# One-hots, sums and node work of a graph kernel moved ahead of VectorE's wait for the gathered rows

## The chip, the cores and the metric

The kernel runs on one core of a Trainium2 chip. The metric is the device time of one execution in microseconds (us); the median of three runs is shown, and one more execution was taken by the hardware profiler. Engines: TensorE (PE, its weight loads PEld), VectorE (DVE), ScalarE (ACT), GpSimd (POOL), and SyncE (SP), which issues most DMAs.

## The reference, cut to what matters

6250 nodes with 128 features, 200000 edges sorted by destination. Two layers, each on the layernorm of the features, each added to them:

```python
h = relu(layernorm(x))
# layer 0: graph attention, 4 heads of 32
xp = h @ W;  e = leaky_relu(a_s[src] + a_d[dst], 0.2)
m = segment_max(e, dst);  e = exp(e - m[dst])
out = segment_sum(e * xp[src], dst) / segment_sum(e, dst)
x = x + relu(out + bias)
# layer 1: edge features and neighbour sums
h = relu(layernorm(x))
edge_agg = segment_sum(edge_attr @ We + be, dst)
x_comb = concat([h, edge_agg]);  neigh = segment_sum(x_comb[src], dst)
x = x + relu((x_comb + neigh) @ W1 + b1) @ W2 + b2
```

The self loops of layer 0 are in the start values of the sums.

## The kernel before, in words

A preparation (0 to 126 us) makes a table of `xp` with its logits in DRAM. Then a loop over 87 groups of 2304 edges (128 partitions by J = 18), two buffers, the same `item(n, b, it)` written once for each engine. Last comes a phase of 49 windows that multiplies an adjacency matrix with the projected nodes (from 2668 us), which the change does not touch.

In one group the engines do this:

- GpSimd gathers the rows of the 2304 sources with 18 indirect DMAs (line 816) into `V[b]`. It runs one group ahead of the others, but holds back by itself (`yield_to_chain`, line 788): ahead of gather 6 it waits for the carry matmul of the group before, ahead of 8 for the peaks (`mg_b`), ahead of 11 for the lookup, ahead of 14, 15 and 16 for the three thirds of the weighted sums (`vm_b`).
- VectorE waits for the 18 gathers (line 1637) and starts the chain of the group, which makes the running maximum per destination: copy of the logits (1638), scan `pre1` (1643), a transpose by TensorE (1142), scan `tails` over the partitions (1651), a matmul back (1144), carry (1660), scan `pre2` (1664), peaks (1671), split of them into three bf16 parts (`split_peaks`, 1507 to 1513). TensorE multiplies the peaks with the one-hots `selH` (1161, 18 matmuls). VectorE makes the new maximum and the shift of the window's 128 nodes out of it (1689 to 1717), also split in parts. TensorE looks the shift up for each edge (1177, 18 matmuls), VectorE forms the exponent (1725 to 1737), ScalarE the exponential (949), VectorE multiplies the rows with it in three parts (1742), TensorE sums them (1194).
- `select` (1479, 1491) makes `selH`, the one-hots of each edge's node in its window, for the sums; it waits until the one-hots of the group before have been used. ScalarE copies them to float32 (`SEL`, line 933), behind its evacuation of three adjacency blocks, and TensorE takes them for the sums of the edge features (1133: three of the eighteen ahead of the lookup, the rest behind it) and of the rows (1194).
- `rescale_state` and `add_sums` (1523, 1533) take the sums of the window before to the new maximum and add the group's; they wait for the load of the window's sums, for the fold factor and for the last third of the matmuls. SyncE then stores the sums (509).
- `finish_weights` to `finish_shift` (1543 to 1610) are some twenty small steps of the nodes of the group before (m = n - 1): mean, bias, residual, layernorm with a Newton square root. Each waits for the one before (`done`). `finish_projection` (1612) evacuates the projection of the group n - 2; it waits for its matmuls and until the store of the projection before has landed (`y_out`), since both use the tile `fy`. Before, these steps stand one by one between the chain's steps.
- `edge_marks` (1493) make one-hots for the adjacency matrix, which TensorE multiplies (1123, 1125) and ScalarE evacuates; SyncE stores 1568 KB of it for each group (526).

SyncE's queue of a group n, in order: store of the sums n - 1, store of the peaks n, loads of the indices n + 2, of peaks and rows n + 1, of the edge features n + 2 (1152 KB, line 453, after the edge-feature sums of n), of the sums n (502, after the transposes of window n - 1), of x (505), stores of the residual n - 1 (515), of the projection n - 2 (520), of the adjacency n - 1 (526).

The order of work is written out by hand; engines meet only through semaphores.

Of the kernel before, what the change touches and what calls it, by code (L numbers as in the profile page):

```python
# [14 lines left out]
H = 4  # L15
# [37 lines left out]
NK = 3  # L53
# [28 lines left out]
def gnn_kernel(nc, x, src, dst, attr, W, att_src, att_dst, bias0, We, be, W1, b1, W2, b2, out):  # L82
    ctx = ExitStack()
    with ctx:
# [81 lines left out]
        step = sb("step", [128, RT])  # L166
# [133 lines left out]
        def s(name):  # L300
            if name not in S:
                S[name] = sem(name)
            return S[name]
# [980 lines left out]
        def _(dve):  # L1284
# [194 lines left out]
            def select(n, b, extra_group=None):  # L1479
                after(dve, s("mg_b"), n, 1)  # L1480
                after(dve, s("selc_b"), n, 1)
                if extra_group is None:
                    at = drp[:, bass.DynSlice(n, 1), :].rearrange("p a j -> p (a j)")
                else:
                    v.tensor_scalar(drxp[b][:, :].rearrange("p (j e) -> p j e", e=2),
                                    dd[:, bass.DynSlice(extra_group, 1), :].rearrange("p a (j e) -> p (a j) e", e=1)
                                    .to_broadcast([128, J, 2]), exto[:, bass.DynSlice(n - NG, 1)], None,
                                    ALU.subtract).then_inc(s("drx_b"), 1)
                    dve.wait_ge(s("drx_b"), n - (NG - 1))
                    at = drxp[b][:, :]  # L1490
                equal(selH, J, WIN, at).then_inc(s("sel_b"), 1)
# [41 lines left out]
            def add_sums(n, b):  # L1533
                dve.wait_ge(s("vm_b"), n * QN + QN)
                dve.wait_ge(s("ms_b"), n * 2 + 2)
                v.tensor_tensor(state[:, :], state[:, :], pv[b][:, 0:ST], ALU.add).then_inc(s("merged"), 1)
# [82 lines left out]
            def item(n, b, it, g=None):  # L1619
# [5 lines left out]
                def between(step, *more):  # L1625

                    if m is not None:
                        step(m, *more)
# [7 lines left out]
                                -BIG, None, ALU.mult).then_inc(s("cont_b"), 1)  # L1636
                dve.wait_ge(s(f"gat{b}"), it * 16 * J + 16 * J)
# [8 lines left out]
                select(n, b, extra_group)  # L1646
                if m is not None:
                    rescale_state(m, 1 - b)
# [4 lines left out]
                if m is not None:  # L1653
                    add_sums(m, 1 - b)
                if not (is_extra or (isinstance(n, int) and n < 2)):
                    finish_projection(n - 2)
                between(finish_weights)
                between(finish_mean)
# [3 lines left out]
                between(finish_bias)  # L1662
# [4 lines left out]
                between(finish_residual)  # L1667
                last = isl[:, bass.DynSlice(g, 1), :].rearrange("p a (j c) -> p (a j) c", c=1)
                v.tensor_copy(peaks[:, :, NK * H:NK * H + 1], last).then_inc(s("pkl_b"), 1)
# [3 lines left out]
                between(finish_stats)  # L1673
                split_peaks(n, 0)
                between(finish_variance)
                split_peaks(n, 1)
                between(finish_eps)
                split_peaks(n, 2)
                between(finish_halve)
                split_peaks(n, 3)  # L1680
                between(finish_guess)
# [3 lines left out]
                between(finish_b2)  # L1685
                between(newton_square, 0)
# [6 lines left out]
                between(newton_factor, 0)  # L1693
# [5 lines left out]
                between(newton_step, 0)  # L1699
# [5 lines left out]
                between(newton_square, 1)  # L1705
# [3 lines left out]
                between(newton_factor, 1)  # L1709
                split_shift(n, b, 0)  # L1710
                between(newton_step, 1)
                split_shift(n, b, 1)
                between(newton_square, 2)
                split_shift(n, b, 2)
                between(newton_factor, 2)
# [3 lines left out]
                between(newton_step, 2)  # L1719
                between(finish_shift)  # L1720
# [172 lines left out]
```

## Time and profile before

| | us |
| --- | --- |
| median of 3 runs | 3113.4 (3105.56 to 3114.23) |
| profiled execution, own time | 3102.13 |
| its span | 3100.2 |
| PE busy | 2043.0 (66%) |
| PE weight loads busy | 1674.9 (54%) |
| DVE busy | 1807.2 (58%) |
| ACT busy | 1085.6 (35%) |
| POOL busy | 1673.2 (54%) |

The profile is one execution. Busy times are shares of the span; no engine is near all of it. Times in a timeline are from the start of the span. "Idle before" is the time in which an engine did nothing just ahead of an instruction, with the one that ended it. The granted clock (PEclk) is a share of 2.4 GHz. The ends of matmuls are modelled.

### The profile page before, as it was taken

The page shows a single profiled execution, that of the slowest core. Times are in us where ns is not written, and L with a number is a line of the kernel's source. Part 1 is how long each engine was busy: PE and PEld are TensorE (multiplying, and loading weights), DVE is VectorE, ACT ScalarE, POOL GpSimd, SP SyncE. Part 2 cuts the span into 40 slices and gives each one's busy share as a digit, 9 for nine tenths or more (in the row PEclk, how much of TensorE's full clock was granted, in tenths as well). Part 3 has the DMA queues.
Part 4 walks back from the last instruction along what each step waited for, and adds up shares of the span by engine and source line. Part 5 has one row for each costly group of instructions (what it writes and reads, how often), then busy time and mean ns, then how long its engine had stood idle before and what let it go on. Part 6 is the DMA issues. An engine that isn't in the chain of part 4 may idle for free.

```text
span 3100.2 us, 64216 instructions
## 1 busy us (share of the span) xinstructions
PE 2043.0 (66%) x16208; PEld 1674.9 (54%) x16208; DVE 1807.2 (58%) x6198; ACT 1085.6 (35%) x2295; POOL 1673.2 (54%) x1626
## 2 busy tenths in 40 slices
PE   4365665665665655665656656656656656699998
PEld 3354554554554544554545545545545544588887
DVE  7566676665666666666666766766766766411111
ACT  3134344344434443443443443443444443300000
POOL 4566666666666666666666666666666666000000
PEclk8677777776777767777767777777777777799999
DMA  9855655655655555655556556556556555666654
GB/s 192 134 163 177 194 168 174 195 159 180 193 155 187 177 169 189 189 160 185 162 176 194 157 184 194 168 173 194 156 185 194 156 185 176 225 213 214 225 212 146
DMA packets 276907, 560.29 MB, mean 181 GB/s; under 512 B 113395, under 2 KB 211139, under 8 KB 248081
## 3 DMA queue, kind: packets, MB, share of 16 engines
q1 hardware_dynamic: 226763, 444.37, 42.5%
q0 software_dynamic: 50112, 115.56, 16.5%
q8 instruction: 12, 0.20, 0.0%
q14 instruction: 20, 0.16, 0.0%
HBM read 382.53 MB, written 177.22 MB: 181 GB/s over the span
## 4 chain that ended last, share of the span: by engine, by line
PE 41%; issue 20%; DVE 15%; DMA 9%; another core or an unknown queue 5%; SPq 3%; ACT 2%; POOL 2%; ACTq 1%; DVEq 1%; POOLq 0%
PE pv L1133 10%; PE pv L1248 9%; DMA big<-table,idx 8%; PE pv L1194 7%; PE pt L1248 4%; PE pt L1123 3%; PE pm L1161 2%; POOL big L816 2%; ACT xsb L852 2%; PE pa L1123 1%; DVE peaks L1513 1%; DVE tabb L1477 1%; PE pa L1177 1%; ACTq L905 1%
## 5 line engine op out<-in xcount | busy, mean ns | idle before, releaser
L816 POOL DMA_INDIRECT big<-table,idx x1566 | 1639.8, 1047 | 929.9 <-issue 414.2
L852 ACT ACTIVATE xsb<-pt 128x343 f32 x1042 | 477.8, 459 | 1213.3 <-PE pt L1125 567.1
L1133 PE MATMUL pv<-big 128*128 128x128 f32 x3132 | 523.6, 336 | 5.7 <-ACT big L852 3.5
L1133 PEld LDWEIGHTS pv<-big 128*128 128x128 f32 x3132 | 490.3, 246 | 36.1 <-issue 11.7
L1123 PE MATMUL pt<-tabb 128*128 128x343 bf16 x1042 | 400.0, 384 | 65.8 <-ACT xsb L852 36.5
L1194 PE MATMUL pv<-big 128*128 128x133 f32 x3132 | 391.3, 280 | 7.0 <-DVE big L1742 4.2
L1638 DVE COPY logit<-big 128x72 f32<-128x72 f32 x87 | 21.9, 252 | 608.6 <-DMA big<-table,idx 540.1
L1194 PEld LDWEIGHTS pv<-big 128*128 128x128 f32 x3132 | 367.8, 190 | 16.2 <-DVE big L1742 8.6
L1477 DVE TENSOR_TENSOR tabb<-iotah,keyp 128x2064 bf16<-128x2064 bf16 x261 | 319.7, 1225 | 0.0
L1142 PE MATMUL pm<-ident,pre 128*4 128x128 f32 x87 | 32.5, 374 | 433.9 <-DVE pre L1643 226.5
L1248 PE MATMUL pv<-big,xsb 128*128 128x384 bf16 (+1 forms) x1617 | 279.3, 330 | 18.5 <-DVE big L1779 18.5
L852 ACT ACTIVATE xsb<-pa 128x343 f32 x521 | 238.9, 458 | 95.0 <-ACT xsb L852 50.3
L1248 PEld LDWEIGHTS pv<-big,xsb 128*128 128x128 bf16 (+1 forms) x1617 | 230.4, 147 | 52.4 <-issue 21.4
L1142 PEld LDWEIGHTS pm<-ident,pre 128*4 128x4 f32 x87 | 7.2, 82 | 451.5 <-DVE pre L1643 236.4
L1742 DVE TENSOR_TENSOR big<-big,pm 128x768 f32<-128x768 f32 x261 | 233.4, 949 | 26.2 <-ACT pm L852 18.7
L1125 PE MATMUL pt<-tabb 128*128 128x49 bf16 x1041 | 224.9, 216 | 0.0
L1123 PE MATMUL pa<-tabb 128*128 128x343 bf16 x521 | 200.8, 385 | 28.3 <-issue 18.3
L1161 PE MATMUL pm<-peaks,selb 128*128 128x13 bf16 x1566 | 56.2, 174 | 228.8 <-DVE peaks L1513 143.7
L1123 PEld LDWEIGHTS pt<-tabb 128*128 128x128 bf16 x1042 | 114.9, 110 | 159.5 <-ACT xsb L852 63.1
L1161 PEld LDWEIGHTS pm<-peaks,selb 128*128 128x128 bf16 x1566 | 48.5, 105 | 261.2 <-DVE peaks L1513 157.2
L852 ACT ACTIVATE big<-selb 128x2304 f32<-128x2304 bf16 x87 | 184.1, 2116 | 1.0 <-DVE selb L1477 1.0
L852 ACT ACTIVATE fhT<-pt,b1s 128x128 f32<-128x128 f32 (+1 forms) x49 | 18.0, 367 | 388.6 <-PE pt L1225 388.6
(289 smaller groups left out, 2975.8 us busy)
## 6 DMA issues: line engine op xcount, KB each, us to landing
adj<-xsb SPq DMA_DIRECT2D x87, 1568.0 KB
big<-in_edge_attr_dram SPq DMA_DIRECT2D x87, 1152.0 KB
xsb<-adj SPq DMA_DIRECT2D x33, 1568.0 KB, 6.2
selb<-rel SPq DMA_DIRECT2D x87, 576.0 KB
tabb<-adj SPq DMA_DIRECT2D x16, 1568.0 KB, 6.2
big<-table,idx POOLq DMA_INDIRECT x1566
state<-sums SPq DMA_DIRECT2D x87, 130.5 KB
sums<-state SPq DMA_DIRECT2D x87, 130.5 KB
```

The source lines that it names most:

```text
L816: pool.indirect_dma_start(out=V[b][:, j, 0:rows], out_offset=None, in_=table, in_offset=bass.IndirectOffsetOnAxis(ap=index[b][:, j:j + 1], ...
L852: return nc.scalar.activation(out_, in_, func, **kw).then_inc(s(name), 1)
L905: _, at = nc.values_load_multi_w_load_instructions(offs[0:1, bass.DynSlice(n * OW + lo, hi - lo)], engines=[mybir.EngineType.Activation], ...
L1123: ins = nc.tensor.matmul(pab[c % 3], ohl[:, c, :], ohk[:, c, 0:KW], start=True, stop=alone)
L1125: ins = nc.tensor.matmul(pab[c % 3][:, 0:NB], ohl[:, (c - 1) % J, :], ohc[:, (c - 1) % J, 0:NB], start=False, stop=True)
L1133: ins = nc.tensor.matmul(sumA[b], SEL[b][:, j, :], AT[b][:, j, :], start=(j == 0), stop=(j == J - 1))
L1142: nc.tensor.transpose(tailT, pre1[:, :, J - 1], ident[:, :]).then_inc(s("tailT_b"), 1)
L1161: ins = nc.tensor.matmul(mg, selH[:, j, :], peaks[:, j, :], start=(j == 0), stop=(j == J - 1))
L1194: ins = nc.tensor.matmul(sumV[b], SEL[b][:, j, :], V[b][:, j, 0:TAB], start=(j == 0), stop=(j == J - 1))
L1248: ins = nc.tensor.matmul(pay[k][0:rows, 0:NK * C], adjT[k][:, 0:rows, h], yb[:, h, :], start=(h == 0), stop=(h == NB - 1))
L1477: return v.tensor_tensor(to.rearrange("p j (w e) -> p j w e", e=2), v_in, at, ALU.is_equal)
L1742: v.tensor_tensor(v4, v4, wps[:, js, :].rearrange("p j (h a) -> p j h a", a=1) .to_broadcast([128, QUART, H, F]), ALU.mult).then_inc(s("vw ...
```

## The change

In VectorE's `item`, the one-hots, the copy of the last flags, the rescaling and adding of the sums of the group before, the projection and all the finishing steps are taken out of the chain and stand in one block ahead of the wait for the gathered rows. The chain's own instructions and their order, and the programs of the other engines, stay as they are.

```diff
                                 -BIG, None, ALU.mult).then_inc(s("cont_b"), 1)
+                select(n, b, extra_group)
+                last = isl[:, bass.DynSlice(g, 1), :].rearrange("p a (j c) -> p (a j) c", c=1)
+                v.tensor_copy(peaks[:, :, NK * H:NK * H + 1], last).then_inc(s("pkl_b"), 1)
+                if m is not None:
+                    rescale_state(m, 1 - b)
+                    add_sums(m, 1 - b)
+                if not (is_extra or (isinstance(n, int) and n < 2)):
+                    finish_projection(n - 2)
+                for step in (finish_weights, finish_mean, finish_bias, finish_residual, finish_stats,
+                             finish_variance, finish_eps, finish_halve, finish_guess, finish_b2):
+                    between(step)
+                for r in range(3):
+                    between(newton_square, r)
+                    between(newton_factor, r)
+                    between(newton_step, r)
+                between(finish_shift)
                 dve.wait_ge(s(f"gat{b}"), it * 16 * J + 16 * J)
...
-                select(n, b, extra_group)
-                if m is not None:
-                    rescale_state(m, 1 - b)
                 after(dve, s("thru_c"), n)
                 after(dve, s("tailT_b"), n)
...
-                if m is not None:
-                    add_sums(m, 1 - b)
-                if not (is_extra or (isinstance(n, int) and n < 2)):
-                    finish_projection(n - 2)
-                between(finish_weights)
-                between(finish_mean)
                 after(dve, s("cback_b"), n)
...
-                between(finish_bias)
...
-                between(finish_stats)
                 split_peaks(n, 0)
-                between(finish_variance)
                 split_peaks(n, 1)
...
-                between(newton_step, 2)
-                between(finish_shift)
```

## Rows read from the trace of the kernel before

**Rows 1.** The page's costliest groups: line, engine, tiles, count | busy, mean | idle before.
```profile
L1638 DVE COPY logit<-big 128x72 f32<-128x72 f32 x87 | 21.9, 252 | 608.6 <-DMA big<-table,idx 540.1
```
**Rows 2.** Source view of line 1638: durations in ns, first and last start in us.
```profile
L1638 DVE COPY logit<-big x87: 211/220/455, 126.2 to 2633.2; 128x72 f32<-128x72 f32 x87
```
**Rows 3.** Timeline of a period's first part: start, duration in us, engine, line, tiles.
```profile
1528.42 0.22 DVE L1638 COPY logit<-big 128x72 f32<-128x72 f32 x1 [8.10 <-DMA big<-table,idx]
...
1528.98 1.34 DVE L1477 TENSOR_TENSOR selb<-iotah,drp 128x2304 bf16<-128x2304 bf16 x1
1529.12 0.38 PE L1142 MATMUL pm<-ident,pre 128*4 128x128 f32 x1 [5.24 <-DVE pre L1643]
...
1530.51 0.40 DVE L1651 TENSOR_TENSOR_SCAN tails<-thruT,pm 4x128 f32<-4x128 f32 x1
...
1530.97 0.59 PE L1144 MATMUL pm<-ident,tails 4*128 4x4 f32 x2 [1.48 <-issue]
...
1533.82 2.12 ACT L852 ACTIVATE big<-selb 128x2304 f32<-128x2304 bf16 x1
...
1534.29 0.65 PE L1161 MATMUL pm<-peaks,selb 128*128 128x13 bf16 x18 [1.63 <-DVE peaks L1511]
...
1536.18 1.62 PE L1133 MATMUL pv<-big 128*128 128x128 f32 x6 [0.24 <-ACT big L852]
...
1538.29 0.66 PE L1177 MATMUL pa<-node,selb 128*128 128x24 bf16 x18 [0.49 <-DVE node L1511]
...
1539.76 4.87 PE L1133 MATMUL pv<-big 128*128 128x128 f32 x30
```
**Rows 4.** Timeline of the same and the next period: GpSimd's gathers, SyncE's issues, VectorE's wait.
```profile
1529.27 1.88 POOL L816 DMA_INDIRECT big<-table,idx  x1 [0.30 <-issue]
...
1547.21 0.33 SPq L502 DMA_DIRECT2D state<-sums  x1
...
1549.79 0.18 DVE L1635 TENSOR_SCALAR cont<-isl 128x68 f32 x1
...
1549.87 0.35 SPq L520 DMA_DIRECT2D sums<-fy  x1
...
1550.77 0.94 POOL L816 DMA_INDIRECT big<-table,idx  x1 [0.37 <-issue]
...
1551.19 0.33 SPq L526 DMA_DIRECT2D adj<-xsb  x1
...
1557.36 0.22 DVE L1638 COPY logit<-big 128x72 f32<-128x72 f32 x1 [7.39 <-DMA big<-table,idx]
```
**Rows 5.** Windows: stretch, length, busy of the engines, PEclk, DMA share, GB/s.
```profile
1527.00:1541.00 14.00, 8.04 (x69) 5.75 (x70) 10.84 (x51) 5.46 (x9) 9.91 (x9) 0.50 0.36 75
1549.00:1557.00 8.00, 2.80 (x22) 1.56 (x20) 0.98 (x4) 4.01 (x10) 6.12 (x6) 0.94 1.01 390
```
**Rows 6.** Timeline of the first group, which has no node work.
```profile
128.46 0.58 PE L1144 MATMUL pm<-ident,tails 4*128 4x4 f32 x2 [0.83 <-DVE tails L1651]
129.09 0.22 DVE L1660 SCALAR_TENSOR_TENSOR logit<-pm,cin,logit 128x4 f32<-128x4 f32 x1 [0.68 <-PE pm L1144]
...
131.25 0.63 PE L1161 MATMUL pm<-peaks,selb 128*128 128x13 bf16 x18 [2.20 <-DVE peaks L1513]
```
**Rows 7.** Groups by line of VectorE from 1499 to 2601 us, 38 periods.
```profile
L1689 DVE TENSOR_SCALAR pen<-pm 128x1 f32<-128x1 f32 x38 | 6.0, 157 | 26.2 <-remote 14.3 <-PE pm L1161 11.3
```
**Rows 8.** Timeline behind the last group: adding, projection and finishing with no chain between.
```profile
2653.21 0.43 DVE L1536 TENSOR_TENSOR state<-state,pv 128x261 f32<-128x261 f32 x1 [2.44 <-PE pv L1194]
2653.55 0.34 DVE L1616 SCALAR_TENSOR_TENSOR fy<-bew,fdeg,pa 128x128 f32<-128x128 f32 x1
...
2658.28 0.16 DVE L1609 SCALAR_TENSOR_TENSOR fnm<-fmv,fy 128x1 f32<-128x1 f32 x1
```
**Rows 9.** Tile view of `state`: landing of its loads whose landing the trace has.
```profile
DMA to landing us min/median/max: 1.7/5.4/12.2
```
**Rows 10.** Timeline of another group: the same thirty attribute rows.
```profile
2617.80 3.59 PE L1133 MATMUL pv<-big 128*128 128x128 f32 x30
```

More of the change, by code:

```diff
@@ L1666, in item @@
                     .then_inc(s("pre2_b"), 1)
-                between(finish_residual)
-                last = isl[:, bass.DynSlice(g, 1), :].rearrange("p a (j c) -> p (a j) c", c=1)
-                v.tensor_copy(peaks[:, :, NK * H:NK * H + 1], last).then_inc(s("pkl_b"), 1)
                 after(dve, s("pre2_b"), n)
@@ L1672, in item @@
                                 last.to_broadcast([128, J, H]), ALU.mult).then_inc(s("pk_b"), 1)
-                between(finish_stats)
                 split_peaks(n, 0)
-                between(finish_variance)
                 split_peaks(n, 1)
-                between(finish_eps)
                 split_peaks(n, 2)
-                between(finish_halve)
                 split_peaks(n, 3)
-                between(finish_guess)
                 if not is_extra:
@@ L1684, in item @@
                     v.tensor_scalar(selT, selT, ranko[:, 0:1], None, ALU.is_equal).then_inc(s("selt_b"), 1)
-                between(finish_b2)
-                between(newton_square, 0)
                 after(dve, s("mg_b"), n)
@@ L1692, in item @@
                                 AX.X, ALU.add).then_inc(s("mgs_b"), 1)
-                between(newton_factor, 0)
                 dve.wait_ge(s("st_load"), n * 32 + 32)
@@ L1698, in item @@
                     .then_inc(s("mnew_b"), 1)
-                between(newton_step, 0)
                 after(dve, s("mnew_b"), n)
@@ L1704, in item @@
                                 ALU.add).then_inc(s("nu_b"), 1)
-                between(newton_square, 1)
                 after(dve, s("nu_b"), n)
@@ L1708, in item @@
                                        op0=ALU.mult, op1=ALU.max).then_inc(s("sh_b"), 1)
-                between(newton_factor, 1)
                 split_shift(n, b, 0)
-                between(newton_step, 1)
                 split_shift(n, b, 1)
-                between(newton_square, 2)
                 split_shift(n, b, 2)
-                between(newton_factor, 2)
                 split_shift(n, b, 3)
```

## The prediction, made before the change was run

> **What bounds the kernel now.** I read the costliest groups first. VectorE's copy of the gathered logits (line 1638) has the largest idle time that an engine spends ahead of one VectorE line: 608.6 us over 87 groups, 7.0 us a group, nearly all of it until the gather landed [rows 1]. So VectorE, busy 58% of the span, is no bound by its sum. Then the source view of that line: its first and last starts are 126.2 and 2633.2, so 86 periods take 2507.0 us, 29.15 us each [rows 2]. The rest of the span (preparation, adjacency phase) is not touched.
>
> Then the timeline of one period. The rows land, VectorE starts the chain (logit, scan, TensorE round trip, tails, round trip, carry, scan, split), TensorE multiplies the peaks (1161), VectorE finishes the shift, TensorE looks it up (1177), weights follow, sums follow, and GpSimd is allowed its last two gathers only behind those sums. In the period from 1528.42 to the next logit copy at 1557.36 the reader is to see three stretches: 9.87 us to TensorE's lookup (1177 at 1538.29), 11.4 us to the end of VectorE's own list (mask of line 1635 at 1549.79), and 7.6 us in which VectorE waits [rows 3, 4]. That last stretch is a DMA stretch: the 16 engines are at a share of 1.01 and 390 GB/s from 1549 to 1557, with the adjacency store issued at 1551.19 [rows 4, 5]. The period is a closed loop: what leaves the first stretch shortens it, and what is put into the last is free only up to 7.6 us and only if its inputs are there.
>
> **The first stretch without the moved work.** Now: copy 1528.42, the transpose (1142) 0.70 later, tails at 2.09, the back matmul (1144) at 2.55, 1161 at 5.87 [rows 3]. Between the transpose's end (1.08) and the tails stand the one-hots (1.34 us) and the rescaling. Without them the tails wait only for the transpose. The first group gives the delay: it has no node work, and its carry starts 0.63 after a 0.58 us matmul row, 0.05 after the end [rows 6]. So tails at 1.08 + 0.05 = 1.13; back matmul 0.46 later (as now) 1.59; carry 0.63 later 2.22; and 1161 starts 131.25 - 129.09 = 2.16 after the carry in that first group: 4.38. The gain there is 5.87 - 4.38 = 1.49 us. Of this the one-hots and rescaling are 0.96; the some twenty small steps give only the rest, because each stood in the gap in which the next step of the chain waited for the one before. I take nothing for the Newton steps behind the peaks for that reason (bounds: nothing, and 0.16 us each for the last two, ahead of the edge marks, which the wait for the lookup covers anyway).
>
> The lookup has a second path. ScalarE's copy of the one-hots (2.12 us) started 2.85 behind the back matmul (1533.82), because the evacuation of three adjacency blocks stands ahead of it; then six attribute rows (1536.18) and the lookup [rows 3]. It moves by 0.96 only: copy at 4.44, attribute sums 2.36 later at 6.80, lookup at the earliest 1.62 later at 8.42. By the VectorE path it is 9.87 - 1.49 = 8.38. So the lookup starts at 8.42, and **1.4 us** are gained. Making the one-hots sooner doesn't help that copy: it is held by what stands ahead of it on ScalarE.
>
> Bounds: VectorE also waits ahead of line 1689, 26.2 us over 38 groups, 0.69 us each, partly for nothing that the view names [rows 7]. If such waits end at fixed moments and so fill up what the chain gives, the floor is 1.4 - 0.7 = 0.7 us; if they vanish, the gain is 1.4 + 0.7 = 2.1 us. I keep them as they are.
>
> **The last stretch with the moved work.** Ahead of the wait now come one-hots, copy of the last flags, rescaling, adding, projection, finishing, shift. The end of the last group shows this block alone: adding 2653.21, projection 2653.55, shift 2658.28 with 0.16 [rows 8], so 5.2 us from adding, 4.9 from projection to the end; every step waits for the one before with nothing between. One-hots and rescaling are 1530.51 - 1528.98 = 1.53 us [rows 3]. From 1549.90: adding at 1551.5 at the earliest, all done at 1556.8, 0.6 before the copy at 1557.36. It fits by 0.6 us if nothing is late, but two inputs are young. Rescaling waits for the state load of that group, issued at 1547.21, and the projection waits until the store of the projection before has landed (it shares the tile), issued at 1549.87 [rows 4]. The nearest landing row is that of the state loads: 1.7 least, 5.4 median, 12.2 most [rows 9], the median behind a 1568 KB load. This state load stands behind 1152 KB, which by size makes 5.4 x 1152/1568 = 4.0: 1551.2, in time. For the 64 KB store I take 3 us, nearer to the least, since it stands behind small transfers: 1552.87, projection there instead of 1551.85, block done at 1557.8, the copy 0.4 late. By the bounds the store costs nothing at 1.7 us and 1555.3 + 4.9 = 1560.2, 2.8 us late, at 5.4.
>
> The one-hots now run while GpSimd makes the last two gathers. The row of a gather begun at 1529.27 is 1.88 us long: it ends 0.83 behind the one-hots of 1528.98 to 1530.32, where an undisturbed one takes 0.94 [rows 3, 4]. Moved to 1549.90 to 1551.24 they meet the gather of 1550.77, whose end goes from 1551.71 to 1552.07: 0.36 us (bounds 0 and 0.94). The Trainium skill, page "SBUF — State Buffer", section "Who interferes with whom", has it that a tensor_tensor with both inputs in SBUF only takes the pair's read side and so should leave descriptor making alone (which it calls inferred); by it this term is nothing. The row of 1.88 us is against it, and the sum goes by the row.
>
> SP's queue: the store of the sums (130 KB) leaves at about 1552 instead of 1531, that is into the full stretch. At 390 GB/s its 130 KB add 0.3 us to what has to be drained ahead of the rows. All other SP entries keep their order and gates, since load of sums, residual and projected stores stay behind the attribute load. The gathers' yields to the chain come sooner with the chain; GpSimd has 18 gathers of 0.94 + 0.30 us, 22.5 us, in a period of 28, so it stays under.
>
> These don't add: rows landing 0.4 to 0.6 later (gather and store) and VectorE 0.4 late are the larger of two. With the groups not being alike I take **0.6 us**.
>
> **The sum.** -1.4 + 0.6 = -0.8 us a group, over 86 groups -69 us. The profiled execution took 3102.1 us (3100.2 span), so 3033; the median of the runs shown is 11 us above that execution (3113.4), so 3044, and I say **3042 us**.
>
> **Rivals.**
> 1. The gain is given back: the rows land when the DMA queue is drained, and nothing but the start of that drain counts; or VectorE is late by 1 to 1.4 us. For it: share 1.01 in the stretch. Against: the adjacency store is issued behind attribute sums that shift with the lookup. Time 3113 less 0 to 0.3 x 86 = 3087 to 3113.
> 2. Slower: the projection's wait for the landed store, now ahead of the wait for the rows, decides. Everything of the chain queues behind it on VectorE, and TensorE, ScalarE and GpSimd behind that. Price: each us of landing beyond 2.6 is a us of every group; it decides beyond 2.6 + 1.4 = 4.0 us. At the 5.4 of the landing row [rows 9] the net is 2.8 - 1.4 = +1.4 us, +120 us: 3235; at 4.7, 3173. For it: the full DMA stretch; against: at 64 KB it is small, and the adjacency store is issued only behind it.
> 3. More is gained: the unnamed waits vanish and TensorE's clock rises sooner. From 1527 to 1541 it was granted 0.50 of full speed (1.2 GHz) [rows 5], and the thirty attribute rows took 4.87 us, against 3.59 in another group [rows 3, 10], which an earlier rise to 2.4 GHz would explain. With the first 0.7 and half of the second 1.28 a group gains 1.3 more: 112 us, 2930.
>
> **Chances.** Forecast 0.52 (its own range 2985 to 3085), rival 1 0.16, rival 2 0.14, rival 3 0.18. Less than 0.3% (9 us) can't be told from no change. Rival 1 is half faster, half same: faster 0.52 + 0.18 + 0.07 = 0.77, same 0.08, slower 0.15 (rival 2 and a late tail of rival 1). The range takes the forecast, rival 1 and the nearer half of rival 3: 2955 to 3120.
>
> **What would show it.** Right: 1161 starts about 4.4 and 1177 about 8.4 behind the logit copy (5.87 and 9.87 now); VectorE's idle ahead of line 1638's copy falls from 7.0 to under 1 us; the shift of line 1609 stands ahead of the copy; some gathers at the end of a group are 1.3 us long; a period near 28.3 us. Wrong: a gap of VectorE ahead of line 1616 (store) or 1528 (state) above 1.5 us and the gather landed well before the copy (rival 2), or the copy still waiting for rows with a period of 29 (rival 1), or full clock before 1177 (rival 3).

## The result and the profile after

The changed kernel takes 3134.61 us (median of 4 runs, 3130.25 to 3141.55), the kernel before 3112.24 us (4 runs, 3105.56 to 3114.23): ratio 1.0077, 95% interval 1.0052 to 1.0103. It is slower by 0.8%, where 3042 us was forecast. Two copies of one kernel, run side by side later, differed by 0.3%; the loss is small but clear of that. The profiled execution took 3130.25 us, its span is 3128.3 us.

The source view of the logit copy, now line 1654 (durations in ns; first and last start in us), answers to [rows 2]:
```profile
L1654 DVE COPY logit<-big x87: 206/220/410, 127.5 to 2662.0; 128x72 f32<-128x72 f32 x87
```
86 periods take 2534.5 us, 29.47 us each, against 29.15: 0.32 us more, 27.5 us in all, which is the whole difference of the spans (28.1 us). So the loss is in this loop.

A period's first part in the timeline, as in [rows 3] (the last brackets give the idle time before the row and what ended it):
```profile
1508.74 0.21 DVE L1654 COPY logit<-big 128x72 f32<-128x72 f32 x1
1509.42 0.37 PE L1142 MATMUL pm<-ident,pre 128*4 128x128 f32 x1 [5.09 <-DVE pre L1659]
1510.37 0.58 PE L1144 MATMUL pm<-ident,tails 4*128 4x4 f32 x2 [0.57 <-issue]
1511.09 0.22 DVE L1667 SCALAR_TENSOR_TENSOR logit<-pm,cin,logit 128x4 f32<-128x4 f32 x1 [0.78 <-PE pm L1144]
...
1513.12 2.12 ACT L852 ACTIVATE big<-selb 128x2304 f32<-128x2304 bf16 x1
1513.18 0.65 PE L1161 MATMUL pm<-peaks,selb 128*128 128x13 bf16 x18 [1.13 <-DVE peaks L1513]
1515.29 1.65 PE L1133 MATMUL pv<-big 128*128 128x128 f32 x6 [0.46 <-ACT big L852]
1516.74 0.16 DVE L1685 TENSOR_SCALAR pen<-pm 128x1 f32<-128x1 f32 x1 [2.91 <-remote]
...
1518.69 0.66 PE L1177 MATMUL pa<-node,selb 128*128 128x24 bf16 x18 [1.76 <-DVE node L1513]
```
The reader is to see that the chain did what it was to do as far as TensorE's peaks' matmuls: 1161 starts 4.44 us behind the logit copy (5.87 before, 4.38 forecast), ScalarE's copy 4.38 (4.44 forecast). Then VectorE waits 2.91 us for a product whose matmuls were over at 1513.83, and the lookup starts at 9.95: in this group nothing is left of the 1.43 us.

One group is a sample. The means over the 87 groups, in us behind the logit copy of the same group, say how much came through:

| | before | after | difference |
| --- | --- | --- | --- |
| peaks' matmuls start (1161) | 6.90 | 5.36 | -1.54 |
| penalty starts (1689, after: 1685) | 8.52 | 8.15 | -0.37 |
| lookup starts (1177) | 10.56 | 10.16 | -0.40 |
| VectorE's last instruction ahead of the moved block (mask, 1635) | 21.89 | 21.60 | -0.29 |
| from there to the next logit copy | 7.26 | 7.87 | +0.61 |
| period | 29.15 | 29.47 | +0.32 |

The chain up to the peaks is 1.54 us shorter, three quarters of that are lost ahead of the penalty, 0.29 us are left at the mask, and the longer list behind it costs 0.61.

The waits behind this stand in the groups by line (busy, mean ns | idle before). First of the kernel before, then of the changed kernel:
```profile
L1725 DVE TENSOR_REDUCE lks<-pa 128x144 f32<-128x432 f32 x87 | 52.8, 607 | 69.5 <-remote 68.5 <-PE pa L1177 0.9
L1689 DVE TENSOR_SCALAR pen<-pm 128x1 f32<-128x1 f32 x87 | 13.7, 157 | 66.8 <-remote 40.3 <-PE pm L1161 24.9
```
```profile
L1712 DVE TENSOR_REDUCE lks<-pa 128x144 f32<-128x432 f32 x87 | 52.9, 608 | 98.9 <-remote 98.8
L1685 DVE TENSOR_SCALAR pen<-pm 128x1 f32<-128x1 f32 x87 | 13.8, 159 | 203.1 <-remote 188.5 <-PE pm L1161 14.3
...
L1528 DVE TENSOR_TENSOR state<-state,fold 128x128 f32<-128x128 f32 x87 | 25.4, 292 | 41.3 <-DMA state<-sums 39.1 <-issue 2.1
L1616 DVE SCALAR_TENSOR_TENSOR fy<-bew,fdeg,pa 128x128 f32<-128x128 f32 x87 | 29.9, 344 | 6.5 <-PE pa L1114 2.9 <-DMA sums<-fy 2.5
L1654 DVE COPY logit<-big 128x72 f32<-128x72 f32 x87 | 21.1, 242 | 5.0 <-DMA big<-table,idx 4.1 <-issue 0.6
```
The wait ahead of the penalty grew from 0.77 to 2.33 us a group ((203.1 - 66.8)/87 = 1.57 more), that ahead of the lookup's sums from 0.80 to 1.14. (Before, VectorE still had steps of the nodes to do while TensorE multiplied the peaks, so a part of the same delay did not show as idle time.) VectorE's wait for the rows, 608.6 us before [rows 1], is down to 5.0: what fills it is the moved list, with 0.47 us a group of waiting for the loaded state (41.3/87) in it, and at most 0.07 ahead of the projection (6.5/87, of it 0.03 for the store).

The load of the state, the list's end and the next copy in the timeline (as [rows 4]), and the two windows that answer to [rows 5] (stretch, length, busy of PE, PEld, DVE, ACT, POOL, PEclk, DMA share, GB/s):
```profile
1527.43 0.33 SPq L502 DMA_DIRECT2D state<-sums  x1
...
1530.10 0.19 DVE L1635 TENSOR_SCALAR cont<-isl 128x68 f32 x1
1530.21 1.35 DVE L1477 TENSOR_TENSOR selb<-iotah,drp 128x2304 bf16<-128x2304 bf16 x1
...
1532.59 0.29 DVE L1528 TENSOR_TENSOR state<-state,fold 128x128 f32<-128x128 f32 x1 [0.92 <-DMA state<-sums]
...
1538.14 0.16 DVE L1609 SCALAR_TENSOR_TENSOR fnm<-fmv,fy 128x1 f32<-128x1 f32 x1
...
1538.26 0.24 DVE L1654 COPY logit<-big 128x72 f32<-128x72 f32 x1
```
```profile
1507.00:1521.00 14.00, 7.66 (x67) 5.34 (x68) 8.56 (x33) 5.35 (x9) 9.27 (x10) 0.50 0.32 72
1530.00:1538.00 8.00, 2.57 (x20) 1.35 (x18) 6.38 (x29) 3.64 (x9) 5.67 (x6) 0.74 1.00 370
```
The copy follows the list at once: VectorE is late. From the mask (1530.10) to the copy are 8.16 us, 7.57 before [rows 4]: 0.6 us more, the same as in the means. The rescaling (1528) starts 5.16 us behind the issue of the load that it waits for. VectorE does 2.3 us less in the first window, and the stretch isn't shorter.

### The profile page after: what moved, and what is told of

It is laid out like the page before. It is cut to its first block, busy times and chain, and to the rows that moved or that the text cites. A ratio compares the mean times of both kernels' runs of the same rounds, so it can differ in the third digit from the quotient of the medians.

```text
span 3128.3 us, 64216 instructions
## 1 busy us (share of the span) xinstructions
PE 2081.7 (67%) x16208; PEld 1712.1 (55%) x16208; DVE 2014.1 (64%) x6198; ACT 1078.0 (34%) x2295; POOL 1657.4 (53%) x1626
## 4 chain that ended last, share of the span: by engine, by line
PE 38%; issue 19%; DVE 18%; another core or an unknown queue 9%; DMA 5%; SPq 4%; ACT 4%; ACTq 2%; DVEq 0%; POOL 0%; POOLq 0%
PE pv L1133 11%; PE pv L1248 8%; PE pv L1194 6%; PE pt L1248 4%; ACT xsb L852 3%; DMA state<-sums 2%; PE pt L1123 2%; DVE selb L1682 2%; ACTq L905 1%; DVE tabb L1477 1%; PE pa L1177 1%; PE pa L1123 1%; PE pm L1144 1%; DVE pre L1670 1%
## 5 line engine op out<-in xcount | busy, mean ns | idle before, releaser
L1133 PE MATMUL pv<-big 128*128 128x128 f32 x3132 | 561.3, 353 | 34.3 <-ACT big L852 17.6
L1133 PEld LDWEIGHTS pv<-big 128*128 128x128 f32 x3132 | 527.7, 263 | 70.9 <-issue 34.0
L1194 PEld LDWEIGHTS pv<-big 128*128 128x128 f32 x3132 | 367.9, 190 | 6.4 <-DVE big L1729 2.3
L1779 DVE TENSOR_TENSOR fy<-pa,fxw 128x128 f32<-128x128 f32 (+1 forms) x49 | 14.3, 292 | 227.3 <-PE pa L1232 227.3
```

The lines of the kernel that those rows point to most:

```text
L1133: ins = nc.tensor.matmul(sumA[b], SEL[b][:, j, :], AT[b][:, j, :], start=(j == 0), stop=(j == J - 1))
L1194: ins = nc.tensor.matmul(sumV[b], SEL[b][:, j, :], V[b][:, j, 0:TAB], start=(j == 0), stop=(j == J - 1))
```

## The experiments

They ran in five lots on five different chips, beside the kernel before, which took 2838, 3114, 3170, 3176 and 2848 us there. I call the first and the last the fast chips, the others the slow ones. No chip was used twice, so these runs can't tell the chip from the occasion. Ratios hold within a lot.

**First lot: where the peaks' result is waited for.** GpSimd's pause for that result was moved in both kernels, since it is ahead of gather 8 and the stall ended soon behind gather 7 (where VectorE waited over 0.5 us, 1.9 us behind the gather's end in the median); the one-hots were moved alone; and two Newton rounds were left out of the changed kernel (the reciprocal root is then less exact).
```diff
 # after_y4, before_y4: yield_to_chain
-                if j == 6:
-                    pool.wait_ge(s("cback_b"), n)
-                    pool.sem_inc(s("g_started"), 1)
-                if j == 8:
+                if j == 4:
                     pool.wait_ge(s("mg_b"), n)
 # sel_only: before, with only this moved
+                select(n, b, extra_group)
                 dve.wait_ge(s(f"gat{b}"), it * 16 * J + 16 * J)
 ...
-                select(n, b, extra_group)
 # after_newton1: FIN = 12
-                for r in range(3):
+                for r in range(1):
```


> The changed kernel with GpSimd's yield for the peaks put ahead of gather 4 instead of gather 8 (and the carry's yield dropped, which it implies), so that far fewer gathers are in flight while TensorE multiplies the peaks. In the changed kernel line 1161 starts 5.4 us (least 4.33) after the logit copy, and VectorE's line 1685 that takes its result starts at 8.2, though the matmuls are 0.65 us long. Theory A, the gathers in flight hold back what the engines tell each other: line 1685 comes down to 5.6 to 6.2 us after the copy, and the period falls from 29.5 by 1 to 2 us (time 2960 to 3060). Theory B, the result is late for a reason of TensorE's own (its clock, its weight loads) : line 1685 stays at 8 to 8.3 and the time stays within 10 us of 3135 or goes up. Theory C, ScalarE's copy of the one-hots out of the tile that TensorE reads: the same as B here, since the copy stays at 4.4 to 6.5.

> The same shift of the yields in the kernel before. Line 1161 starts at 6.95 us on average (least 5.85) and line 1689 at 8.55. Theory A: line 1689 falls to 7.0 to 7.3 and the period by about 1 us, time near 3030; with the moved block still in the chain it stays above the changed kernel with the same yields by the 1.4 us a group that I had predicted. Theories B and C: line 1689 stays at 8.5, the time within 10 us of 3112 or above.

> The kernel before with one part of the change: only the one-hots (select) stand ahead of the wait for the rows, everything else stays in the chain. It takes 1.3 us out between pre1 and tails and adds nothing that waits for a landing, and VectorE's block ahead of the wait is 1.3 us in 7.6. Theory A (the end of the peaks' wait is set from outside the chain): line 1161 starts about 1 us sooner, line 1689 hardly moves (8.2 to 8.5), and the time is 3090 to 3115, less than the changed kernel's because VectorE is not late for the rows. Theory B (the chain sets it): 3020 to 3050.

> The changed kernel with one Newton round instead of three (two rounds of the square root are left out), so its block ahead of the wait is six dependent steps, 1.27 us, shorter. If VectorE's lateness for the rows (copy 1.18 us after the gather's store has landed, 0.62 before the change) is what made the change a loss, the idle time ahead of the logit copy comes back (0.3 to 0.6 us a group), the period falls by 0.4 to 0.6 us and the time to 3085 to 3100, below the kernel before. If the DMA queue alone sets the landing, the time stays within 10 us of 3135.

Measured, before at 2837.52 us: after_y4 2943.62 us, ratio 1.038 (1.036 to 1.041); before_y4 3007.02, 1.061 (1.058 to 1.063); sel_only 2762.65, 0.973 (0.971 to 0.976); after_newton1 2828.7, 0.998 (0.996 to 0.999). The surprise is the chip: the same kernel is 9% faster there, and VectorE has no stall ahead of the penalty in any of the four traces. Groups by line of sel_only:
```profile
L1689 DVE TENSOR_SCALAR pen<-pm 128x1 f32<-128x1 f32 x87 | 13.1, 150 | 0.0
```
So this lot could not test the stall; it shows that the moved pause makes the gathers late where there is nothing to repair, and that the one-hots alone are worth 2.7% there.

**Second lot: the parts, and both kernels again.** The finishing steps moved and the one-hots left in the chain (fin_ahead); one-hots, rescaling and adding moved and the finishing steps left (sel_sums).
```diff
 # fin_ahead: after, with
-                select(n, b, extra_group)
                 last = isl[:, bass.DynSlice(g, 1), :].rearrange("p a (j c) -> p (a j) c", c=1)
 ...
+                select(n, b, extra_group)
                 after(dve, s("thru_c"), n)
 # sel_sums: before, with ahead of the wait for the rows (and not behind it)
+                select(n, b, extra_group)
+                last = isl[:, bass.DynSlice(g, 1), :].rearrange("p a (j c) -> p (a j) c", c=1)
+                v.tensor_copy(peaks[:, :, NK * H:NK * H + 1], last).then_inc(s("pkl_b"), 1)
+                if m is not None:
+                    rescale_state(m, 1 - b)
+                    add_sums(m, 1 - b)
```


> The kernel before, unchanged, for its own trace on this chip. Its ratio is 1.000 under either theory. Theory A (the 1.4 us that the chain gained up to the peaks' matmuls is swallowed by stalls of several engines between the peaks' first matmul and the penalty on VectorE): if the time is near 2838 us, the stalls are absent from its trace (VectorE waits under 0.3 us for the peaks' result, the penalty starts 0.7 to 1.0 us after the peaks' first matmul, against 1.6 us in the trace of the prediction); if it is near 3112 us they are there. Theory B (the swallowing is a wait of this program for a fixed event, whatever the condition): the distance stays 1.6 us at any time.

> The changed kernel, unchanged. Theory A: where before takes near 2838 us there is no stall that could swallow the 1.4 us; the peaks' result is used 1.0 to 1.5 us earlier in the group, and what decides is only how late VectorE's longer list ends before the rows: with 0.6 us of lateness at its end the ratio is 0.97 to 0.99; where before takes near 3112 us it is 1.008 again. Theory C (VectorE's list of 18 steps and their writes end so late that the transfers and the matmuls behind them, and with them the last gathers, land 1 us late as well): the ratio is 1.00 to 1.02 on either chip, and the wait for the rows starts no earlier than before.

> The changed kernel with the one-hots back in the group's chain, behind the first scan (about 0.9 us of VectorE's chain); rescaling, sums and all finishing steps stay ahead of the wait. The select's move alone gave 0.973. Theory C (the list's length decides): this kernel's list ends 1.4 us sooner than after's, so it is 0.5 to 1.0% faster than the changed kernel. Theory A: the moves add up, so it is slower than the changed kernel by what the one-hots cost in the chain, 0.5 to 0.9 us a group, 1.5 to 2.5%.

> The one-hots, the last-column copy, the rescaling and the adding of sums ahead of the wait; the finishing steps of the last group stay between the chain's steps, as in the kernel before. Theory A: the steps that leave the chain are 4 of some 0.1 us each, so it is 0.3 to 1% faster than the move of the one-hots alone (0.973), unless the wait for the state's rows ends behind the gathered rows. Theory C: sums made sooner bring the writes forward and leave the list 1.5 us shorter than after's, ratio 0.96 to 0.975, clearly under the changed kernel.

Measured, before at 3113.8 us: before_same 3119.9 us, 1.003 (1.001 to 1.005), so 0.3% is what two copies of one kernel differ by; after_same 3134.07, 1.008 (1.006 to 1.011), the result again; fin_ahead 3145.09, 1.009 (1.005 to 1.013); sel_sums 3130.66, 1.008 (1.005 to 1.011). Every version that shortens the chain ends in the same place; neither theory had that, since C wanted both parts under the changed kernel and A wanted fin_ahead 1.5% or more above it. In sel_sums TensorE's peaks' matmuls start 4.7 us behind the copy, and one group shows who waits (timeline):
```profile
1515.72 0.65 PE L1161 MATMUL pm<-peaks,selb 128*128 128x13 bf16 x18 [1.33 <-DVE peaks L1513]
...
1516.88 0.94 POOL L816 DMA_INDIRECT big<-table,idx  x1 [0.31 <-issue]
...
1519.53 0.16 DVE L1688 TENSOR_SCALAR pen<-pm 128x1 f32<-128x1 f32 x1 [2.75 <-remote]
...
1519.67 0.46 ACT L852 ACTIVATE xsb<-pt 128x343 f32 x1 [2.10 <-remote]
...
1520.28 0.94 POOL L816 DMA_INDIRECT big<-table,idx  x1 [2.46 <-remote]
```
VectorE, ScalarE and GpSimd all wait for products of TensorE that were finished 1516.4 to 1517.4, and all go on within 0.8 us. It is the word of the finished work that comes late, not the work. What it waits for there the trace doesn't say ("remote" stands where it has no record of the event).

**Third lot: a fixed amount of events, or the gathers?** SyncE got 24 idle increments a group.
```diff
                     store_sums(n - 1, base_before)
+                    for _ in range(24):
+                        sp.sem_inc(s("sp_turn"), 1)
                 store_peak(n, b, base)
```


> The kernel before with 24 extra semaphore increments a group on SyncE, that nobody waits for, put where SyncE waits 5.8 us a group for the new peaks (506.2 us over 87 groups in the trace of before). They cost the data path nothing if each takes under 0.1 us. Theory D (where before takes near 3112 us, the stalls of several engines are set by a fixed amount of events that a group produces, such as semaphore updates and instruction ends, and not by the kernel's chain): the time rises there, by 1% or more, while where before takes near 2838 us it stays within 0.3%. Theory E (the stalls come from gathers in flight): no change within 0.3% on either.

> The move of the one-hots alone, again. It gave 0.973 where before takes near 2838 us. Theory A (the chip's condition swallows what the chain gains up to the peaks): 0.973 again where before takes near 2838 us, and 1.00 to 1.01 where it takes near 3112 us, with VectorE waiting 2 us or more for the peaks' result. Theory F (the longer list alone decides, and the one-hots alone are a gain anywhere): 0.97 to 0.98 on either.

> The changed kernel, unchanged, again. It gave 1.008 where before takes near 3112 us. Where before takes near 2838 us: theory A says 0.975 to 0.99 (no stall to swallow the gain, 0.5 to 1.0 us a group given back by the list's late end); theory C (the list's late end gives the whole gain back) says 1.00 to 1.01; its cut to one Newton round gave 0.998 there, so I take 1.00 to 1.01 for likelier.

> The changed kernel with GpSimd's wait for the peaks' result moved from ahead of gather 8 to ahead of gather 4, and its wait for the carry left out, again. It gave 1.038 where before takes near 2838 us, with the gathers late. Where before takes near 3112 us: theory E (gathers in flight hold up the peaks' result) says that the penalty starts within 1.5 us of the peaks' first matmul (3.0 us in the changed kernel's trace), ratio 0.99 to 1.02; theory D (a fixed amount of events a group) says that the group's period stays near 29.2 to 29.6 us, ratio 1.00 to 1.015, since the gathers' own bound of 27.3 us lies below it.

Measured, before at 3169.6 us: before_spinc 3178.07 us, 1.003 (1.001 to 1.005), no more than a copy of the kernel differs, so theory D is wrong at the size that it named; sel_only_2 3140.79, 0.991 (0.989 to 0.993); after_same_2 3153.48, 0.994 (0.992 to 0.997); after_y4_2 3461.08, 1.093 (1.091 to 1.095). On this chip the change is a small gain, and the one-hots alone a larger one. Theory A missed here too: it wanted 1.00 or more for the one-hots, with a wait of 2 us for the peaks' result, which was 0.95 us (82.8/87). after_y4_2 lies 7% above the range that I gave, but its rows say where the stall is. Groups by line:
```profile
L1709 DVE TENSOR_REDUCE lks<-pa 128x144 f32<-128x432 f32 x87 | 52.8, 607 | 187.9 <-remote 184.4 <-issue 3.5
L1682 DVE TENSOR_SCALAR pen<-pm 128x1 f32<-128x1 f32 x87 | 13.8, 159 | 2.6
```
With GpSimd halted ahead of gather 4 the wait ahead of the penalty is gone (2.6 us, 181.3 in after_same_2), and that ahead of the lookup's sums grew from 104.3 to 187.9 us: GpSimd now runs through ten gathers there (4 to 13). The stall went where the gathers went, but it doesn't last until they are over: of the 71 groups in which VectorE waits over 0.5 us ahead of the lookup's sums, 69 end their wait in the middle of a gather, and GpSimd gathers on. Ahead of the penalty GpSimd waits for the same word as VectorE, so that it has stopped there doesn't show that the stop ends the stall.

**Fourth lot: the run of gathers made shorter and longer.** The pause ahead of gather 6, and in after_late none until the one ahead of gather 11 (the wait for the carry ahead of 6 stays there, but gather 6 starts 1.28 us behind gather 5 in the mean, as without a wait).
```diff
 # before_y6, sel_y6, after_y6
                 if j == 6:
-                    pool.wait_ge(s("cback_b"), n)
-                    pool.sem_inc(s("g_started"), 1)
-                if j == 8:
                     pool.wait_ge(s("mg_b"), n)
 # after_late
-                if j == 8:
-                    pool.wait_ge(s("mg_b"), n)
-                    pool.sem_inc(s("g_started"), 1)
```


> The kernel before with one pause of GpSimd for the peaks' result, ahead of gather 6 (before: for the carry ahead of 6, for the peaks' result ahead of 8). Theory E (a run of gathers without a pause holds up all engines): where before takes 3112 us or more, the penalty starts 0.7 to 1.5 us behind the peaks' first matmul (1.6 us in before) and that matmul near 6.0 us, so the chain up to it is 1 to 1.5 us shorter, and gather 8 starts at about 9.3 us as before; ratio 0.96 to 1.00, less if a new stall comes behind the lookup. Theory G (the stall has its place for another reason): the penalty stays at 8.5 us and the gathers are 2 us later, ratio 1.02 to 1.06. Where before takes near 2838 us there is no stall, the gathers bound: 1.01 to 1.04.

> The same pause with the one-hots ahead of the wait for the rows. Theory E: where before takes 3112 us or more, the penalty at 5.7 to 6.5 us against 8.7 us, gather 8 at 8.5 us against 9.4 us, ratio 0.94 to 0.98, the fastest of the four. Theory G: the penalty stays past 8 us, ratio over 1.00. Where before takes near 2838 us: 0.97 to 1.00, against 0.973 with the pauses as they were.

> The same pause in the changed kernel. Theory E: where before takes 3112 us or more, the penalty at 5.1 to 5.8 us against 8.3 us in the changed kernel's trace, gather 8 at 8.0 us against 9.0 us, the rest of the group's chain 1 us or more ahead of it; the list that ends late then costs what it was to cost, so ratio 0.95 to 0.99. Theory G: the penalty stays past 8 us, ratio over 1.01. Where before takes near 2838 us: 1.00 to 1.03.

> The changed kernel without GpSimd's pause for the peaks' result: it gathers on to number 11, where it waits for the lookup's matmuls. Theory E: where before takes 3112 us or more, the stall lasts until gather 10 is done, so the penalty starts at 10 to 12 us against 8.3 us and the ratio is 1.02 to 1.08. Theory G: the penalty stays at 8.3 us and the gathers are earlier, ratio 0.97 to 1.00. Where before takes near 2838 us: no stall, gathers earlier, 0.96 to 1.00.

Measured, before at 3175.89 us: before_y6 3234.2 us, 1.017 (1.013 to 1.021); sel_y6 3179.17, 1.001 (1.000 to 1.003); after_y6 3367.48, 1.060 (1.056 to 1.065); after_late 3524.94, 1.109 (1.105 to 1.113). Idle of VectorE ahead of the penalty, groups by line of before_y6, sel_y6, after_y6 and after_late in this order:
```profile
L1686 DVE TENSOR_SCALAR pen<-pm 128x1 f32<-128x1 f32 x87 | 13.2, 151 | 1.5 <-remote 1.2 <-PE pm L1158 0.2
```
```profile
L1686 DVE TENSOR_SCALAR pen<-pm 128x1 f32<-128x1 f32 x87 | 13.2, 152 | 0.3 <-PE pm L1158 0.2
```
```profile
L1682 DVE TENSOR_SCALAR pen<-pm 128x1 f32<-128x1 f32 x87 | 13.8, 159 | 102.4 <-remote 54.9 <-PE pm L1158 46.9
```
```profile
L1682 DVE TENSOR_SCALAR pen<-pm 128x1 f32<-128x1 f32 x87 | 13.8, 158 | 578.7 <-remote 576.4 <-PE pm L1158 2.2
```
In the changed kernel that is, by the gather ahead of which GpSimd pauses, 0.03 us a group (4), 1.18 (6), 2.08 to 2.33 (8, three traces) and 6.65 (none until 11); with the one-hots alone 0.00 (6) and 0.95 (8), in the kernel before 0.02 (6) and 0.74 to 0.77 (8). A group of after_late, timeline and windows:
```profile
1527.76 0.65 PE L1158 MATMUL pm<-peaks,selb 128*128 128x13 bf16 x18 [3.85 <-DVE peaks L1510]
...
1530.22 0.94 POOL L813 DMA_INDIRECT big<-table,idx  x1 [0.30 <-issue]
1533.66 0.16 DVE L1682 TENSOR_SCALAR pen<-pm 128x1 f32<-128x1 f32 x1 [6.36 <-remote]
...
1533.80 0.46 ACT L849 ACTIVATE xsb<-pt 128x343 f32 x1 [6.69 <-remote]
```
```profile
1528.60:1533.60 5.00, 2.27 (x12) 1.69 (x10) 0.00 (x0) 0.00 (x0) 1.96 (x3) 0.50 0.19 44
```
For 5 us VectorE and ScalarE do nothing at all, until 2.5 us behind the end of the last gather that GpSimd could issue (1531.16). Theory E holds for the direction and the place: in the means the penalty starts 6.90, 6.18, 6.94 and 13.29 us behind the copy in these four kernels, in that order, where theory G wanted 8 or more with the pause ahead of 6. Its times failed: all four ratios lie above the ranges that I gave, and with the pause ahead of 6 they are near those of theory G. So the stall ahead of the penalty can be taken away, but no version without it was faster. One cause is that the pause costs gather time: gather 6 of the next group starts 7.4 us behind the copy in before_y6 and 4.5 in before_same (means). The other is that waits come back behind the lookup. In sel_y6 VectorE is idle for 165.0 us ahead of edge marks, and in after_y6 for 178.8 ahead of the lookup's sums (104.3 in after_same_2) and ahead of the weighting of the rows (32.3 in after_same_2) for
```profile
L1726 DVE TENSOR_TENSOR big<-big,pm 128x768 f32<-128x768 f32 x261 | 233.5, 950 | 239.6 <-ACT pm L849 180.6 <-issue 59.0
```
Why after_y6 keeps half of its wait ahead of the penalty, where the other two lose it, is not settled; its gathers run 1.5 us later against the copy than those of sel_y6 (number 5 at 3.8 and 2.2 us).

**Fifth lot: the rest of the chain, on a fast chip.** `j == 8` became `j == 7` in sel_only and in the changed kernel.

> The one-hots ahead of the wait, GpSimd's pause for the peaks' result ahead of gather 7 instead of 8. Theory E: one gather fewer in the run, so where before takes 3112 us or more the penalty starts at 6.0 to 7.5 us (8.7 us with the pause ahead of 8, 6.2 us ahead of 6) and gather 8 starts at 8.0 to 9.2 us against 9.4 us; if the gain comes through, ratio 0.96 to 0.985; if what is behind the lookup takes it, 0.985 to 1.00 (0.991 with the pause ahead of 8, 1.001 ahead of 6). Where before takes near 2838 us: 0.97 to 0.99.

> The changed kernel with the same pause. The chain up to the peaks' matmul is 0.5 us shorter than in sel_y7, the list behind it ends some 1.5 us later. If the list's late end decides, it is 0.5 to 2% slower than sel_y7 on the same chip, ratio 0.985 to 1.01; if it does not, it is as fast or faster. Where before takes near 2838 us: 1.00 to 1.02.

Measured, before at 2847.94 us: sel_y7 2785.93 us, 0.978 (0.974 to 0.981); after_y7 2856.33, 1.003 (1.001 to 1.005). Both had been expected within these bounds. There is no stall (0.1 and 2.1 us over all groups ahead of the penalty), so this pair shows alone what the list of sums and finishing costs ahead of the wait: 2.5%, 0.77 us a period. TensorE's rows of a group, sel_y7 (logit copy at 1506.8) and then after_y7 (1523.25):
```profile
1511.76 0.65 PE L1161 MATMUL pm<-peaks,selb 128*128 128x13 bf16 x18 [1.63 <-DVE peaks L1513]
1513.65 1.62 PE L1133 MATMUL pv<-big 128*128 128x128 f32 x6 [0.24 <-ACT big L852]
1515.06 0.68 PE L1177 MATMUL pa<-node,selb 128*128 128x24 bf16 x18
1516.56 3.67 PE L1133 MATMUL pv<-big 128*128 128x128 f32 x30
```
```profile
1527.77 0.65 PE L1161 MATMUL pm<-peaks,selb 128*128 128x13 bf16 x18 [1.05 <-DVE peaks L1513]
1529.95 1.65 PE L1133 MATMUL pv<-big 128*128 128x128 f32 x6 [0.54 <-ACT big L852]
1531.39 0.68 PE L1177 MATMUL pa<-node,selb 128*128 128x24 bf16 x18
1532.89 4.47 PE L1133 MATMUL pv<-big 128*128 128x128 f32 x30
```
The peaks come 0.6 us sooner, ScalarE's copy doesn't, so TensorE idles ahead of the attribute rows: over all groups 57.3 us against 9.3. Lookup and attribute rows start no sooner, and the thirty rows take 0.80 us longer. The windows show the clock at that (columns: busy of PE, PEld, DVE, ACT, POOL, then PEclk; the thirty rows begin in the second of each pair):
```profile
1513.80:1515.80 2.00, 2.00 (x25) 1.85 (x26) 1.88 (x14) 1.57 (x4) 1.70 (x2) 0.50 0.55 55
1515.80:1517.80 2.00, 2.00 (x16) 1.69 (x15) 1.97 (x5) 1.20 (x3) 1.67 (x2) 0.77 0.36 65
```
```profile
1530.20:1532.20 2.00, 2.00 (x26) 1.80 (x27) 2.00 (x5) 1.44 (x5) 1.45 (x2) 0.50 0.33 25
1532.20:1534.20 2.00, 2.00 (x12) 1.72 (x11) 1.59 (x6) 1.31 (x4) 1.70 (x2) 0.50 0.70 212
```
Without the hole the granted clock leaves 0.50 (1.2 GHz) within the stretch from 9 to 11 us behind the copy; with it, it is still there. It is so over all groups: the clock first rises 10.06 us behind the copy in the mean in sel_y7 and 11.52 in after_y7. That the hole postpones the rise is my reading; no run filled the hole alone. What is behind it is late in turn: the transpose of the finished nodes (line 1108) starts 13.3 and 14.0 us behind the copy in these two groups, and in the mean as well; SyncE's load of the state is queued behind that, and VectorE's rescaling, now ahead of the wait for the rows, waits for it 98.4 us (0.0 in sel_y7). From the mask to the next copy are 8.69 us in the mean, 6.96 in sel_y7; that is 1.73 us lost where the chain had brought 0.96 (mask at 17.54 and 18.50). The rows are late too: gather 17 starts 21.88 us behind the copy, 21.41 in sel_y7. after_newton1 fits this: its list was shorter, and VectorE waited 114.0 us for rows.

## Why the prediction was wrong

**The step that failed** is "so the lookup starts at 8.42, and 1.4 us are gained", and in it "I keep them as they are" of the unnamed waits ahead of line 1689. They are one stall of several engines whose end did not move with the chain: the peaks' matmuls start 1.54 us sooner in the mean, and 1.18 of it is lost between them and the penalty. The lookup gained 0.40 us, the mask 0.29. The text had the right words for it ("if such waits end at fixed moments and so fill up what the chain gives") but let them eat no more than their present length, 0.69 us. That was the mistake: a wait that ends at a fixed moment grows by what is gained ahead of it, so its present length is no bound, and the floor of the gain was 0 and not 0.7. With the measured terms the sum is -0.29 + 0.61 = +0.32 us a period, 27.5 in all.

**Up to the peaks' matmuls** the working held: 1161 at 4.44 (4.38) and ScalarE's copy at 4.38 (4.44) in the group shown, and a gain of 1.54 us in the mean where 1.49 was forecast. But the group that was read for it had little of the waits (1161 at 5.87 and the lookup at 9.87, in the mean 6.90 and 10.56). On the fast chips, where the stall is absent, the second path decides as the text says: the lookup starts at 8.16 us in sel_y7 and in after_y7, though the peaks come 0.6 us sooner in the latter.

**The late list** came out in size (0.61 us, 0.6 forecast), and that is luck, since its terms did not. The store ahead of the projection was to cost 0.4; it costs at most 0.07. The load of the state was to take 4.0 us, and so be in time; in the group shown the rescaling starts 5.16 us behind its issue, and the wait costs 0.47 us a group. The 5.4 us from which the 4.0 was worked out belong to 64 KB loads of the last phase (line 597); the trace of before has no landing of the loop's own 130 KB loads.

**The gathers beside the one-hots**: one of the last two of a group was to be 0.36 us longer. Gather 16 takes 1.16 us in the mean, 0.94 before, and 17 stays as it was (0.96, 0.94), so the term was there with 0.22, and the other reading that the prediction names, by which it is nothing, is not borne out. Gathers 3 and 4, beside which the one-hots ran before, fell from 1.11 and 1.18 to 0.95, and so the mean of all gathers fell from 1.047 to 1.037. Here the term costs nothing, since VectorE is later than the rows.

**Small slips** of the working change nothing in its result: the second stretch is 11.50 us and not 11.4, the moved block would have been done at 1556.7 and not 1556.8, and 18 gathers of 1.24 us are 22.3 us and not 22.5.

**Rival 1** (the gain is given back) came nearest in its result, though not by the DMA queue, and its 3087 to 3113 us is too low. **Rival 2** (the projection's wait) named the right side by the wrong wait: 6.5 us in all. **Rival 3** had the clock's sign wrong: from 1507 to 1521 it is 0.50 as before, it first rises 14.22 us behind the copy in the mean (13.65 before), and the attribute rows, of 336 ns and 523.6 us in all before, take more, not less. The page's row after:
```profile
L1133 PE MATMUL pv<-big 128*128 128x128 f32 x3132 | 561.3, 353 | 34.3 <-ACT big L852 17.6
```

**What the sign hangs on** is the chip, or the occasion: 1.008 at 3114 us, 0.994 at 3170 us. The changed kernel with its own pause was not run on a fast chip; with the pause ahead of gather 7 it is 1.003 there. The best version is the one-hots alone: 0.973 and 0.991, below the kernel before in both lots, and 0.4% below the changed kernel in the one in which both ran, little more than copies differ by. It was not run on the chip of 3114 us; sel_sums, its nearest kin there, is 1.008.

**Open**: by what way the gathers hold up the word of finished work, what ends the stall, and why on some chips only. 24 more events of SyncE a group don't do it. That it has to do with how an execution is recorded is a rival that these runs leave standing, and one figure speaks for it: the traces from the slow chips hold 186 to 251 records of semaphore updates for each group, those from the fast chips 577 to 586, of nearly the same programs. All times here are of executions that were recorded, so none shows the kernel without it.

## What to carry to other kernels

Ask of each wait on the chain what ends it: if the end does not move with the chain (here its place followed where GpSimd pauses among its gathers), time gained ahead of it is mostly lost (here 1.18 of 1.54 us), whatever its present length. When one engine's work moves forward, look at the engine that gets its product: a product that comes before its other input opens a hole. And of a block that is to be hidden under a wait, move only the part whose inputs are long there: the one-hots needed nothing late and paid, the sums and the finishing needed a load just issued and did not.

## What the runs showed of the hardware

- One kernel took 2838, 3112, 3114, 3170, 3176 and 2848 us in the six lots of this study (five of them on five different chips, of the one at 3112 us the chip isn't known); copies in one lot differed by 0.3%. A change of 1% can change sign between lots.
- On the slow chips the wait of VectorE, ScalarE and GpSimd for the word of TensorE's finished work depends on where GpSimd pauses among its gathers: in the changed kernel VectorE's wait for the peaks' result is 0.03 us a group with the pause ahead of gather 4, 1.18 ahead of 6, 2.1 to 2.3 ahead of 8, 6.65 with none until 11. On the fast chips it is 0.00 to 0.03 with the pause ahead of 4, 7 or 8.
- A hole of about 0.55 us a group on TensorE ((57.3 - 9.3)/87) went with a granted clock that first rose 11.52 us behind the logit copy instead of 10.06, and with thirty attribute rows of 4.47 instead of 3.67 us in the groups shown.
- In the changed kernel the 149 gathers that run beside VectorE's one-hots (line 1477, bf16, 128x2304) for 0.3 us or more take 1.43 us in the mean, the others 1.00.
